# Who begins the experts' transfers: the sync queue or ScalarE, in the tail of a two-layer kernel

## The reference

```
h = exp(dt_t[..., None] * A) * h + (dt_t * u_t)[..., None] * B_t[:, None, :]   # recurrence, 16 states
y_t = einsum('bdn,bn->bd', h, C_t)
idx = argmax(hn2 @ gate_w + gate_b, axis=-1)                                   # one expert per token
mid = relu(einsum('th,ehf->etf', hn2, w1) + b1);  y = einsum('etf,efh->eth', mid, w2) + b2
moe = y[idx, arange(tokens)]                                                   # 128 -> 512 -> 128
```

## Time and profile before

| what | us |
|---|---|
| median of three runs | 1499.34 |
| the profiled execution's own time | 1494.55 |
| its span | 1492.8 |
| DVE, PE, ACT, POOL busy over the span | 1241.4, 994.9, 865.8, 514.5 |
| issues of expert weights and biases (23 slots, four each), and of results (23) | all by SP |

### The profile page before, as it was taken

The page is one execution under the profiler, slowest core; times in us unless marked ns, Lnnn a source line. Parts: engine busy times, 40 slices in busy tenths (PEclk is TensorE's granted clock), DMA queues, the critical chain, the costliest instruction groups (busy, mean ns, idle before and its releaser), DMA issues. The chain is left out here.

```text
span 1492.8 us, 18241 instructions
## 1 busy us (share of the span) xinstructions
PE 994.9 (67%) x5865; PEld 327.3 (22%) x5865; DVE 1241.4 (83%) x1874; ACT 865.8 (58%) x1286; POOL 514.5 (34%) x472
## 2 busy tenths in 40 slices
PE   1439997888888888888888886243275555542444
PEld 0124331111111111111111112021043333310111
DVE  7975466899999999999999932899996666798996
ACT  3134557677777777777777786243454444553441
POOL 2311021300000000000000000698995666799894
PEclk7769996899999999999999998555566767675555
DMA  3004242300000000000000003764857675795530
GB/s 88 0 3 159 107 171 107 105 13 1 1 26 26 1 1 7 21 25 2 1 1 2 1 1 73 165 134 102 199 122 172 143 171 139 169 188 112 113 85 29
DMA packets 88785, 111.42 MB, mean 75 GB/s; under 512 B 15539, under 2 KB 46042, under 8 KB 88690
## 3 DMA queue, kind: packets, MB, share of 16 engines
q1 hardware_dynamic: 87666, 108.16, 29.1%
q0 software_dynamic: 1024, 2.10, 0.5%
HBM read 84.36 MB, written 25.56 MB: 74 GB/s over the span
## 5 line engine op out<-in xcount | busy, mean ns | idle before, releaser
L768 DVE TENSOR_REDUCE at_mpart<-psum 128x1 f32<-128x512 f32 x1024 | 637.8, 683 | 52.5 <-PE psum L915 49.2
L744 ACT ACTIVATE at_probs<-psum 128x1024 f32<-128x1024 f32 x512 | 495.2, 1021 | 147.3 <-PE psum L943 147.0
L1276 POOL TENSOR_TENSOR t_inject<-t_dus,t_bs 128x512 f32<-128x512 f32 x256 | 320.1, 1276 | 93.3 <-issue 38.9
L1642 PE MATMUL psum<-t_hc,stack 128*32 128x512 f32 x512 | 108.2, 930 | 254.5 <-DVE t_hc L1454 254.3
L956 PE MATMUL psum<-at_probs,at_vg 128*32 128x512 f32 x2048 | 274.7, 608 | 0.5 <-ACT at_probs L744 0.4
L915 PE MATMUL psum<-at_ks,at_qs 56*128 56x512 bf16 x1024 | 203.1, 393 | 94.0 <-DVE at_mpart L768 93.3
L1334 ACT ACTIVATE psum<-t_dts,aneg 128x512 f32<-128x512 f32 x256 | 175.9, 692 | 83.5 <-DVE t_hc L1454 39.3
L640 POOL CAST at_m<-at_mneg 128x16 bf16<-128x16 f32 x16 | 3.1, 196 | 584.3 <-DVE at_mneg L773 572.7
L1531 DVE TENSOR_TENSOR_SCAN psum<-psum,t_last,t_inject 128x512 f32<-128x512 f32 x142 | 178.8, 1277 | 11.9 <-issue 9.5
L943 PE MATMUL psum<-at_qs,at_ks 59*128 59x512 bf16 x1024 | 157.8, 380 | 9.7 <-ACT at_probs L744 8.2
L915 PEld LDWEIGHTS psum<-at_ks,at_qs 56*128 56x128 bf16 x1024 | 49.3, 93 | 424.2 <-DVE at_mpart L768 408.5
(11 more groups left out here) (241 smaller groups left out, 956.8 us busy)
## 6 DMA issues: line engine op xcount, KB each, us to landing
t_dts<-mp_dt_d SPq DMA_DIRECT2D x64, 256.0 KB, 6.1
t_dus<-mp_dtu_d SPq DMA_DIRECT2D x64, 256.0 KB
t_w<-in_w SPq DMA_DIRECT2D x46, 256.0 KB
t_bs<-mp_bc_d SPq DMA_DIRECT2D x128, 64.0 KB
t_cs<-mp_bc_d SPq DMA_DIRECT2D x128, 64.0 KB
mp_u_d<-mp_u SPq DMA_DIRECT2D x8, 512.0 KB, 5.1
mp_z_d<-mp_z SPq DMA_DIRECT2D x8, 512.0 KB, 4.9
mp_dt_d<-mp_soft_dt SPq DMA_DIRECT2D x8, 512.0 KB, 2.9
```

The costliest lines, as they stand in the source:

```text
L744: act.activation(probs[:, u_ % 2, p, :], s_pair[p], ACT.Exp, scale=float(HD) ** -0.5).then_inc(probs_ready, 1)
L768: dve.reduce_max(mpart[:, s % 2, 2 * jp + b, i, kc:kc + 1], ring[x % 3], AX.X).then_inc(ring_free, 1)
L1276: pool.tensor_tensor(inject[:, k % NI, :], dus[:, i % 2, j, :], bs[:, m % NBC, :], ALU.mult).then_inc(injected, 1)
L1642: mm = pe.matmul(y_bank[GC * j:GC * (j + 1), :], S.stack[:, :], hc[:, r % 2, j, :], start=False, stop=(q == NQ - 1), tile_position=(0, GC ...
```

## The change

The two helpers `load_expert` and `store_result` move from the sync engine's stream into ScalarE's, with the same waits and the same transfers. In ACT's loop over tiles the load of the weights of slot r-15 comes after tile j = 1 of round r, behind the hidden layer of slot r-19; the store of slot r-20 comes after tile j = 2, behind the turned rows of slot r-18. The sync engine keeps `load_block`, `load_bc` and `load_rows`.

```diff
         @block.sync
-            def load_expert(s):
-                w = s % W
-                if s == 0:
-                    sp.wait_ge(eid_ready, 1)
-                if s >= W:
-                    sp.wait_ge(side_full, USE["Y", s - W] + 1)
-                e = sp.value_load(eid[0:1, s:s + 1], min_val=0, max_val=NE - 1)
-                sp.dma_start(w1[:, w, :], ...).then_inc(w_ld[w], 16)      # and b1, w2, b2
-            def store_result(s):
-                sp.wait_ge(emptied["act"], EMPTIED[USE["Y", s]][1])
-                sp.dma_start(y_dram[P * s:P * (s + 1), :], y[:, s, :]).then_inc(y_st, 16)
...
-                if (s := slot_at(r, -4)) is not None:
-                    load_expert(s)
-                if (s := slot_at(r, 4)) is not None:
-                    store_result(s)
         @block.scalar
+            def load_expert(s):
+                w = s % W
+                if s == 0:
+                    act.wait_ge(eid_ready, 1)
+                if s >= W:
+                    act.wait_ge(side_full, USE["Y", s - W] + 1)
+                e = act.value_load(eid[0:1, s:s + 1], min_val=0, max_val=NE - 1)
+                act.dma_start(w1[:, w, :], ...).then_inc(w_ld[w], 16)     # and b1, w2, b2
+            def store_result(s):
+                act.wait_ge(emptied["act"], EMPTIED[USE["Y", s]][1])
+                act.dma_start(y_dram[P * s:P * (s + 1), :], y[:, s, :]).then_inc(y_st, 16)
...
                 if m == 1:
                     if (s := slot_at(r - 2, 0)) is not None:
                         hidden(s)
+                    if (s := slot_at(r - 2, -4)) is not None:
+                        load_expert(s)
                 if m == 2:
                     if (s := slot_at(r - 2, -1)) is not None:
                         turned(s)
+                    if (s := slot_at(r - 2, 1)) is not None:
+                        store_result(s)
```

More of the change, by code:

```diff
@@ L1313, in result @@
                 act.activation(y[:, s, :], bank("Y", s)[:, 0:P], ACT.Copy).then_inc(emptied["act"], 1)
+            def load_expert(s):
[5 more added lines that the diff above has]
+                e = act.value_load(eid[0:1, s:s + 1], min_val=0, max_val=NE - 1)
+                act.dma_start(w1[:, w, :], dr["w1"][bass.ds(e, 1)].rearrange("o h f -> h (o f)")).then_inc(w_ld[w], 16)
+                act.dma_start(b1[:, w, :], dr["b1"][bass.ds(e, 1)].rearrange("o p b -> p (o b)")).then_inc(w_ld[w], 16)
+                act.dma_start(w2[:, w, :, :], dr["w2"][bass.ds(e, 1)].rearrange("o (b p) h -> p (o b) h", p=P))\
+                    .then_inc(w_ld[w], 16)
+                act.dma_start(b2[:, w, :], dr["b2"][bass.ds(e, 1)]).then_inc(w_ld[w], 16)
+            def store_result(s):
+                act.wait_ge(emptied["act"], EMPTIED[USE["Y", s]][1])
+                act.dma_start(y_dram[P * s:P * (s + 1), :], y[:, s, :]).then_inc(y_st, 16)
             def backward_out(n):
```

## The result

The changed kernel takes 1576.51 us (median of four, 1575.89 to 1577.11) against 1498.91 us for the kernel before in the same runs: a ratio of 1.052, 95% interval 1.050 to 1.054. The forecast was 1572 us, range 1530 to 1608, slower with a chance of 0.90. Its profiled execution has a span of 1574.2 us, 81.4 more than the 1492.8 before. Two executions of kernels further down were far slower than their neighbours (1731 us with the odd blocks earlier, 4593 us with stores alone); the ratios there leave them out.

The account below looks back on a forecast made before the run. DVE was taken as the bound (83% busy), starved in blocks 5 to 9 by late block loads; 1494.55 + 128 (wait on ScalarE) + 10 (project-outs) + 2 (first loads) - 64 (stalls) = 1571 us, forecast 1572, range 1530 to 1608.

Parts of the forecast that it names:

- What bounds, and what is removed: Blocks 5 to 9: sync queue's waits on results make block data late; moving them takes the whole 63.9 us off.
- The wait on ScalarE as a closed chain: Rounds 19 to 37: ACT's load waits for PE's result, delaying decays, scans, sums and the next load; costs 128 us.
- The turn: One pass DVE, PE, load, decay: 5.5 + 4.8 + 2.7 + 0.8 = 13.8 us at low clock, 13.3 taken.
- the three project-outs: Behind rounds 18, 26 and 34, project-out matmuls stand between sums and result, 3.4 us at high clock: 10 us more.
- The clock: PE's granted clock in the waiting rounds: low level taken in three of four, giving 13.3 us a turn.
- the high-clock sum: One turn with PE at the high clock, PE's part 2.7 us: 11.7 us in place of 13.8.
- Rounds 15 to 18: Loads of slots 0 to 3 have no wait, only 2.7 us each on ACT against about two of slack: 2 us together.
- rival 1: High clock holds (1541 us) or ACT's transfers cost little too (1496); low end within 0.85, far end within 0.04.
- rival 2: ACT's issues slow throughout, 5.0 us a load: 44 us more, 1616 us; chance 0.05.
- rival 3: Wait on ACT is covered, only the gain stays, about 1450 us; needs a turn below 9.9 us; chance 0.06.
- The rule of the Trainium skill on the shared descriptor generator: ACT would stand behind the sync queue's block loads: five loads at 2.3 us more, 11 us, 1582 us.
- The rule of the Trainium skill that several issuing engines save only issue time: By issue time alone 71 us leave the sync queue, nothing gained on the wires; set aside because order was lost.

Follow-up runs that it names:

- the odd blocks earlier: Kernel before with the sync queue loading weights two rounds later, plus odd blocks asked for one round earlier: 1460.97 us, ratio 0.977.
- stores alone: Kernel before with only the result stores moved to ACT, weight loads left on the sync queue: 1493.36 us, ratio 0.999.
- the later loads on the sync queue: Kernel before with the sync queue loading weights two rounds later (slot r-15 in round r), nothing on ACT: 1460.78 us, ratio 0.977.
- five buffers: Changed kernel with five weight buffers in place of four, all 115 transfers still begun by ACT: 1469.93 us, ratio 0.982.
- the wait left with no load behind it: Changed kernel with all waits kept on ACT but the loads of slots 4 to 22 left out: 1523.10 us, ratio 1.019.
- the chain shortened at PE: Changed kernel with PE doing the result of slot r-18 before the sums of round r instead of behind them: 1519.43 us, ratio 1.016.
- the later load: Changed kernel, four buffers, each slot's load one round later on ACT (slot r-16 in place of r-15): 1474.45 us, ratio 0.985.

## Why the prediction was right

- *What bounds, and what is removed.* Stalls of 63.9 us in blocks 5 to 9, from the wait on results in the sync queue, all gone. Shown: by the waits of POOL after, and from the other side by the later loads on the sync queue, which took 194.9 - 156.2 = 39 us of them off without ACT. With five buffers, where the rounds are short, POOL does not wait for block data either.
- *The wait on ScalarE as a closed chain, one turn per round in rounds 19 to 37.* Shown four times: 19 waits of DVE; the wait removed by a buffer; the wait left with no load behind it; the chain shortened at PE. The last gave 1519 where 1520 was expected.
- *The turn.* Forecast 13.3 us, with the three project-outs (10 us) 13.8; measured 14.1. By its terms, as means of the 19 turns: DVE 5.5 (5.5); PE 4.9 (4.8 with the project-outs); the load 2.9 (2.7, of which I had no row on ACT; it was 2.8 in 15 of 23); the decay and the hop 0.8 (0.8). So the path and its parts were right.
- *The clock, and where luck helped.* Of the 19 results awaited 14 took the low-clock 2.08 us and 5 the 1.16, three in four as chosen. But three of the five stand behind project-outs. Only two turns had a shorter PE part, 3.3 and 3.8 us, and none the 2.7 of the high-clock sum: in the 16 turns without a project-out it was 4.65 us where 4.3 was forecast, 6 us too little together. The project-outs made up for it: they cost 5 us together and not 10. The 3.4 us "at the high clock" was a misreading: in that row the granted clock was at the low level from 1166.6 to 1169.4, most of its length. In the changed kernel the clock rose during each of the three, so that most of their matmuls and the result behind them ran at the high level. The turn with the one behind round 26 (granted clock 0.50 from 1213.8 to 1215.7, 1.00 from 1216.8 to 1219.8):

```profile
1213.88 1.94 PE L1642 MATMUL psum<-t_hc,stack 128*32 128x512 f32 x8 [2.87 <-DVE t_hc L1454]
1215.74 2.54 PE L1618 MATMUL psum<-w_out,t_gated 128*128 128x128 f32 x16
1218.21 0.48 PE L1608 MATMUL psum<-t_b,t_every 1*128 1x128 f32 x2
1218.62 1.16 PE L1610 MATMUL psum<-t_w,t_mid 128*128 128x128 f32 x8
```

  The granted clock fell to 0.50 to 0.59 from 0.69 to 0.76, so the longer rounds did cost a second time.
- *The terms that were off.* Rounds 15 to 18 cost 5.8 us in place of 2: with no wait at all, one load took 5.6 us and one 3.8 beside a block load. Rounds 19 to 37 cost 143.5 over 6.55 each, forecast 138. Together that is 9 too little, against 5 of the total (81.4 in the span, 76 forecast); the other 4 are small differences mostly ahead of round 0 and behind round 40, where the change touches nothing.
- *The high clock (rival 1)* held for five results and shortened two turns. *Slow issues throughout (rival 2)* are out: three loads in 23 take more than 3.2 us. *Faster (rival 3)* needed a turn under 9.9 us; the kernels with the wait met are at 164.1 / 19 = 8.6 and are faster, as that bound says.
- *The rule of the Trainium skill on the shared descriptor generator* ("Perfetto Trace Analysis", Per-engine timelines) asked for 11 us more. In the changed kernel stretched issues hardly show, since block loads and ACT's loads fall apart in 14 us rounds. In the kernel with five buffers they meet once a block. ACT's queue there, and the last issues of the sync queue before it:

```profile
1111.04 0.34 ACTq L1301 DMA_DIRECT2D t_w<-in_w  x1
1111.54 1.26 ACTq L1302 DMA_DIRECT2D t_b<-in_b  x1
1112.89 1.19 ACTq L1303 DMA_DIRECT2D t_w<-in_w  x1
```

```profile
1106.75 4.00 SPq L1174 DMA_DIRECT2D t_dus<-mp_dtu_d  x4
```

  There a load takes 4.5 to 5.3 us where its neighbours take 2.8, and even a 2 KB transfer waits, so the cost is not the transfer's own. But a lock held by the sync queue does not account for it: its last issue ended at 1110.75, and ACT's two long ones began at 1111.54 and 1112.89, with none of the sync queue under way until 1119.82. The same holds for one more of the five such loads (slot 13). The 16 DMA engines were 92% busy from 1110.8 to 1114.3. That full engines hold the issue back fits this and is not shown.
- *The rule of the Trainium skill that several issuing engines save only issue time* ("DMA: Bandwidth & Descriptors", Issuing engines are not separate DMA queues). The page calls that time usually small. I set it aside, rightly for the 34 us that the later loads gained, which are order. For the last stalls it was most of the matter, and not small: 6.9 us in a round of 6.55.

## What to carry to other kernels

A transfer that is moved to another engine takes its wait along, and the wait can cost more than the issue. Before a wait goes into the stream of an engine that feeds the bound one, ask how old the awaited event is there, and whether the event itself depends on what stands behind the wait; if it does, the price is a full turn of that loop in every round (here 14.1 us in place of 6.55). Here the two cures were one number each, one more buffer or a later place in the same stream, and the later place was worth most on the queue where the transfers had been all along.

## What the runs showed of the hardware

- ACT begins a transfer in 0.34 to 0.49 us in the turn shown; the sync queue's weight and bias transfers took 0.28 to 0.38 in the later-loads kernel. A register load, four transfers and the gaps hold ACT 2.8 us in 15 of 23 loads, during which no later activation starts.
- An issue on ACT can stretch to between 0.8 and 1.5 us in the kernel with five buffers (1.75 in the changed kernel, 6.80 once with the later load) beside or just behind the sync queue's block loads, also for a 2 KB transfer, and also when the sync queue has no issue under way.
- TensorE's granted clock, 0.69 to 0.76 in 38 us blocks, was 0.50 to 0.59 with the same work in 56 us: the same eight result matmuls took 1.16 us at the one level and 2.08 at the other. In rounds 19 to 37 of the changed kernel it rose to the high level five times, three of them during the 16 matmuls of a project-out.
